# Attention and FFN on one core: score matmuls in two 64-row bf16 tiles, rotating PSUM banks, attention written out

## The chip, the cores and the metric

The program runs on one core of a Trainium2 chip. The metric is device time in microseconds (us). The kernel before takes 944.26 us (median of 3 runs, 941.65 to 945.33).

A core has engines that run side by side: PE (TensorE, matmuls; its weight loads are listed apart as PEld), DVE (VectorE), ACT (ScalarE), POOL (GpSimd) and SP (SyncE, which here only issues DMAs). They meet through semaphores. Matmul results go to PSUM, which has 8 banks of 128x512 f32.

## The reference

One transformer block on x of 32 batches x 256 tokens x 128 features. Attention has 16 heads of 8 features and a distance bias:

```
q, k, v = heads(x @ wq.T), heads(x @ wk.T), heads(x @ wv.T)
attn = softmax(q @ k.T / sqrt(8) - slope[h] * |i - j|)
x = layernorm(x + (attn @ v) @ wo.T + bo)
h = silu(x @ w1.T * s1) * (x @ w2.T * s2)          # 128 -> 512
h = gelu(h @ h1.T * s3); h = gelu(h @ h2.T * s4)   # 512 -> 512
x = layernorm(x + h @ w3.T * s5)
```

## The kernel before

Two stages follow each other: attention over 32 batches, then an FFN over 16 chunks of 512 tokens. The change touches attention alone.

**Stacks.** The scores are matmuls of "stacks". A stack holds for each head a column block whose rows are q and k in split precision (fp32r high and low parts, 3 x 8 rows), rows that build the distance bias, and two rows with the negated maximum of each query. PE projects q and k, ACT and DVE split them into `qk_sb` (the buffer `x_parts` in the profile), SP spills the parts to DRAM (`qk_scratch`) and loads them back as rows of `qk_stack` (L300, L307, L308).

**Two passes per head.** `score_max` (L379, PSUM `ps_a`, 3 banks) makes the scores of the next batch, and DVE takes each query's maximum (L617: a custom add of `corner_rows` with a running minimum, two of 128x256 per head). PE turns the maxima of 8 heads (`turn_max`), ACT and DVE split them (`mrow_hi`, `mrow_lo`), SP writes them as rows of the stack. `score_exp` (L391, `ps_b`, 2 banks) makes the transposed scores of this batch with the maxima subtracted, `add_corner` (L370) adds the part of the bias that the rows can't hold, ACT takes the exponential (L529) into `probs`. `pv` (L406) multiplies 4 heads at once with v in four column tiles of 32; it is fp32 and shows two matmul records per product.

**Order.** It is written out by hand. A step t does 16 slots k: scores-for-maxima of batch t+1, scores-for-exp of batch t, and at the slots in `PE_AT`, `PV_AT`, `ACT_AT`, `DVE_AT` the rest: v projection, q/k projection of batch t+2, turning the output (`turn o`, `turn norm`), `wo`, residual and statistics. `drive` runs steps -2 to 2 written out, 3 to 28 as a loop unrolled by two, the rest written out. POOL adds `bo` and does the layer norm; 11 pieces of FFN weights are split by ACT and DVE during the first and last batches. Two banks `ps_m` serve all these small products.

Of the kernel before, what the change touches and what calls it, by code (L numbers as in the profile page):

```python
# [49 lines left out]
OCOLS = VCOLS // 2  # L50
SLOTS = BLK * HEADS
# [10 lines left out]
STACK = 3 * DH  # L62
MROW = P - 2
KA = MROW
STEPS_T = (MROW - STACK - 4) // BLK // 2 * 2
CORNER = P - STEPS_T
F32_MAX = float(np.finfo(np.float32).max)
QH, QL, KH, KL = range(4)
# [24 lines left out]
ACT_AT = {"max hi 1": 1, "copy o": 2, "v": 3, "qk hi": 4, "max hi 0": 9, "oT": 10}  # L93
DVE_AT = {"max lo 1": 1, "qk lo": 4, "norm": 8, "max lo 0": 10, "res": 13, "stats": 14}
# [7 lines left out]
A_BANK = [1 if h == 3 else (h - 4) % HEADS % 3 for h in range(HEADS)]  # L102


def a_released(b, h):

    before = [g for g in range(h - HEADS, h) if A_BANK[g % HEADS] == A_BANK[h]][-1]
    return b * HEADS + before + 1
# [6 lines left out]

def drive(eng, step, first, loop_from, loop_to, last, unroll):

    for t in range(first, loop_from):
        step(t, t % 2)
    with eng.Fori(0, (loop_to - loop_from) // unroll, 1) as i:  # L120
        for u in range(unroll):
            step(i * unroll + (loop_from + u), (loop_from + u) % 2)
    for t in range(loop_to, last + 1):
        step(t, t % 2)
# [33 lines left out]
def norm_x1(nc, pool, b, par, carried, passed):  # L158
# [3 lines left out]
    wait_apart(pool, carried.stats_done, (b + 1) * BLK, passed)  # L162
# [4 lines left out]
    wait_apart(pool, carried.x1_stored, (b - 1) * DMA, passed)  # L167
# [12 lines left out]

def attention(nc, wts, x, xT, wqT, wkT, wvT, woT, bo, qscale, ident, corner, rows, x1_dram, qk_dram, raw_w, scales,
# [5 lines left out]
    with ExitStack() as ctx:  # L187
# [39 lines left out]
        ps_a = [ctx.enter_context(nc.psum_tensor(f"ps_a{i}", [P, 512], F32)) for i in range(3)]  # L227
        ps_b = [ctx.enter_context(nc.psum_tensor(f"ps_b{i}", [P, 512], F32)) for i in range(2)]
        ps_o = ctx.enter_context(nc.psum_tensor("ps_o", [P, 2, SEQ], F32))
        ps_m = [ctx.enter_context(nc.psum_tensor(f"ps_m{i}", [P, 512], F32)) for i in range(2)]  # L230


        passed = {e: sem(f"passed_{e}") for e in ("sp", "dve", "pool")}
        qk_const_landed = sem("qk_const_landed")
        const_landed = sem("const_landed")
        const_set = sem("const_set")
        rows_landed = sem("rows_landed")
        rows_laid = [sem(f"rows_laid{i}") for i in range(2)]
        v_laid = sem("v_laid")
        xT_landed, x_landed = sem("xT_landed"), sem("x_landed")  # L240
        qk_done, qk_hi, qk_lo = sem("qk_done"), sem("qk_hi"), sem("qk_lo")
        spilled = sem("spilled")
        corner_zero, corner_laid = sem("corner_zero"), sem("corner_laid")
        stacked = [sem(f"stacked{i}") for i in range(2)]
        v_done, v_copied = sem("v_done"), sem("v_copied")
        scores_a, max_done = sem("scores_a"), sem("max_done")
        mT_done, m_hi, m_lo = sem("mT_done"), sem("m_hi"), sem("m_lo")
# [10 lines left out]


        pieces = []  # L260
# [4 lines left out]
        piece_at = [(-2, 8)] * RAW_BUFS + [(0, 11), (1, 11), (2, 11), (BATCH - 3, 11), (BATCH - 2, 11),  # L265
                                           (BATCH - 1, 4), (BATCH - 1, 10)]
        assert len(pieces) == N_PIECES == len(piece_at)

        def pieces_of(t, k):

            return [n for n, (step, head) in enumerate(piece_at) if step == t and k in (None, head)]
# [4 lines left out]
        N_CONST, N_QK_CONST = 5, 3  # L276


        STEPS = dict(first=-2, loop_from=3, loop_to=BATCH - 3, last=BATCH, unroll=2)
        FIRST = STEPS["first"]  # L280

# [764 lines left out]
```

## Time and profile before

| | |
|---|---|
| median of 3 runs | 944.26 us |
| profiled execution, its span | 943.94 us, 942.2 us |
| PE, PEld busy | 892.2 us (95%), 724.7 us (77%) |
| DVE, ACT, POOL busy | 728.5 (77%), 640.1 (68%), 138.3 us (15%) |
| DMA moved | 80.60 MB, mean 86 GB/s |

Busy times are unions of an engine's instructions. A matmul's recorded time holds its pipeline latency, so neighbours overlap, and the distance between the starts of two is what each costs in a stream. The same holds for LDWEIGHTS, DVE and ACT.

### The profile page before, as it was taken

The page shows a single profiled execution, that of the slowest core. Times are in us where ns is not written, and L with a number is a line of the kernel's source. Part 1 is how long each engine was busy: PE and PEld are TensorE (multiplying, and loading weights), DVE is VectorE, ACT ScalarE, POOL GpSimd, SP SyncE. Part 2 cuts the span into 40 slices and gives each one's busy share as a digit, 9 for nine tenths or more (in the row PEclk, how much of TensorE's full clock was granted, in tenths as well). Part 3 has the DMA queues.
Part 4 walks back from the last instruction along what each step waited for, and adds up shares of the span by engine and source line. Part 5 has one row for each costly group of instructions (what it writes and reads, how often), then busy time and mean ns, then how long its engine had stood idle before and what let it go on. Part 6 is the DMA issues. An engine that isn't in the chain of part 4 may idle for free. (4 is left out here: it accounts for less than half of the span.)

```text
span 942.2 us, 23595 instructions
## 1 busy us (share of the span) xinstructions
PE 892.2 (95%) x6786; PEld 724.7 (77%) x6786; DVE 728.5 (77%) x2975; ACT 640.1 (68%) x1136; POOL 138.3 (15%) x213
## 2 busy tenths in 40 slices
PE   2799999999999999999999985999999999999995
PEld 1678878888888888888888863788888888888883
DVE  6788888889888888888988954666677777767664
ACT  5377667666666667666666763677777777777772
POOL 3002121121212112121121312001000000000101
PEclk9799999999999999999999997999999999999998
DMA  6344444344344343444434411001111111111001
GB/s 180 101 116 124 136 112 128 110 113 136 108 130 121 115 126 112 132 113 130 112 112 137 127 48 31 28 23 34 34 33 40 39 45 33 39 39 33 23 23 45
DMA packets 72307, 80.60 MB, mean 86 GB/s; under 512 B 8208, under 2 KB 68368, under 8 KB 69200
## 3 DMA queue, kind: packets, MB, share of 16 engines
q1 hardware_dynamic: 71392, 77.28, 29.1%
q0 software_dynamic: 880, 2.88, 1.0%
q8 instruction: 18, 0.29, 0.1%
q14 instruction: 17, 0.14, 0.0%
HBM read 45.53 MB, written 33.55 MB: 84 GB/s over the span
## 5 line engine op out<-in xcount | busy, mean ns | idle before, releaser
L617 DVE CUSTOM_DVE_ANT_0 scored<-ps_a,corner_rows 128x256 f32<-128x256 f32 x1024 | 376.4, 418 | 16.0 <-PE ps_a L379 6.1
L529 ACT ACTIVATE probs<-ps_b 128x512 f32<-128x512 f32 x512 | 300.0, 598 | 128.0 <-PE ps_b L370 125.7
L379 PE MATMUL ps_a<-qk_stack 126*128 126x256 f32 x1024 | 244.2, 321 | 15.9 <-DMA qk_stack<-qk_scratch 12.8
L391 PE MATMUL ps_b<-qk_stack 128*128 128x256 f32 x1024 | 211.0, 288 | 3.2 <-ACT probs L529 2.4
L379 PEld LDWEIGHTS ps_a<-qk_stack 126*128 126x128 f32 x1024 | 158.9, 193 | 46.5 <-issue 27.4
L391 PEld LDWEIGHTS ps_b<-qk_stack 128*128 128x128 f32 x1024 | 159.0, 191 | 8.3 <-ACT probs L529 4.6
L851 ACT ACTIVATE gelu_f<-ps_r,sc 128x512 f32<-128x512 f32 x128 | 88.2, 689 | 79.9 <-PE ps_r L792 72.4
L406 PE MATMUL ps_o<-probs,v_aug 128*32 128x256 f32 x2048 | 137.0, 385 | 0.4 <-ACT probs L529 0.4
L370 PE MATMUL ps_b<-corner_sb,idr_sb 128*128 128x160 f32 x512 | 122.4, 239 | 0.0
L789 PE MATMUL ps_r<-g1h,h_hi 128*128 128x512 f32 x256 | 102.8, 401 | 1.9 <-DVE g1l L916 1.9
L789 PE MATMUL ps_r<-g2h,h_hi 128*128 128x512 f32 x256 | 102.8, 401 | 0.0
L792 PE MATMUL ps_r<-g1l,h_hi 128*128 128x512 f32 x256 | 102.3, 399 | 0.0
L792 PE MATMUL ps_r<-g2l,h_hi 128*128 128x512 f32 x256 | 101.4, 396 | 0.0
L370 PEld LDWEIGHTS ps_b<-corner_sb,idr_sb 128*128 128x128 f32 x512 | 97.0, 189 | 0.0
L882 DVE TENSOR_TENSOR g2l<-gelu_f,g2h 128x512 fp32r<-128x512 f32 x64 | 44.4, 694 | 59.5 <-ACT g2h L852 59.3
L617 DVE DVE_READ_ACCUMULATOR2_ANT negmax<- 128x1 f32 x1024 | 83.6, 82 | 0.0
L406 PEld LDWEIGHTS ps_o<-probs,v_aug 128*32 128x32 f32 x2048 | 53.4, 109 | 34.3 <-ACT probs L529 0.6
L882 DVE TENSOR_TENSOR g3l<-gelu_f,g3h 128x512 fp32r<-128x512 f32 x64 | 42.9, 690 | 33.6 <-ACT g3h L852 33.6
L163 POOL TENSOR_SCALAR vareps<-meanvar 128x2 f32<-128x2 f32 x32 | 7.3, 228 | 406.7 <-DVE meanvar L647 401.2
L906 DVE SCALAR_TENSOR_TENSOR gate_f<-ps_r,sc,act_f 128x512 f32<-128x512 f32 x64 | 46.0, 749 | 20.8 <-ACT act_f L861 20.3
L789 PEld LDWEIGHTS ps_r<-g1h,h_hi 128*128 128x128 f32 x256 | 48.7, 190 | 14.7 <-DVE g1l L916 3.0
L792 PEld LDWEIGHTS ps_r<-g1l,h_hi 128*128 128x128 f32 x256 | 48.8, 191 | 11.7
(99 smaller groups left out, 1260.5 us busy)
## 6 DMA issues: line engine op xcount, KB each, us to landing
qk_stack<-qk_scratch SPq DMA_DIRECT2D x64, 384.0 KB
qk_scratch<-x_parts SPq DMA_DIRECT2D x32, 512.0 KB, 3.0
qk_scratch<-x_parts SPq DMA_DIRECT2D x32, 256.0 KB, 3.3
xT_sb<-in_xT SPq DMA_DIRECT2D x32, 128.0 KB, 2.1
x_sb<-in_x SPq DMA_DIRECT2D x32, 128.0 KB, 2.5
x_scratch<-x_sb SPq DMA_DIRECT2D x32, 128.0 KB, 1.7
x_in<-x_scratch SPq DMA_DIRECT2D x32, 128.0 KB, 2.1
x_res<-x_scratch SPq DMA_DIRECT2D x32, 128.0 KB, 2.1
```

The costliest lines, as they stand in the source:

```text
L163: nc.gpsimd.tensor_scalar(vareps[:], mv[:, :, 1], EPS, None, ALU.add).then_inc(carried.eps_done, 1)
L370: return pe.matmul(out, idr_sb[:], corner_sb[:], start=False, stop=True, skip_group_check=True)
L379: mm = pe.matmul(ps[:, qb * SEQ:(qb + 1) * SEQ], q_stack[par][0:KA, h, qb * P:(qb + 1) * P], k_stack[par][0:KA, h, :], start=(qb == 0), st ...
L391: pe.matmul(ps[:, kb * SEQ:(kb + 1) * SEQ], k_stack[par][:, h, kb * P:(kb + 1) * P], q_stack[par][:, h, :], start=(kb == 0), stop=False, s ...
L406: mm = pe.matmul(ps_o[VCOLS * g:VCOLS * (g + 1), pack, :], v_flat[:, kb, first:first + VCOLS], probs[:, h % HALF, kb * SEQ:(kb + 1) * SEQ] ...
L529: nc.scalar.activation(probs[:, k % HALF, :], ps_b[k % 2][:], ACT.Exp, scale=slope[k]).then_inc(exp_done, 1)
L617: ins = nc.vector.tensor_tensor_reduce(scored[:, k % 2, qb, :], ps_a[A_BANK[k]][:, qb * SEQ:(qb + 1) * SEQ], corner_rows[:, qb, :], -1.0, ...
L789: pe.matmul(ps[:], w_hi, a_hi, start=(k == 0), stop=False)
L792: mm = pe.matmul(ps[:], w_hi, a_lo, start=False, stop=(k == kt - 1))
L851: nc.scalar.activation(gelu_f[:, o, :], ps_r[o][:], ACT.Gelu, scale=scale)
L882: nc.vector.tensor_tensor(lo[:, o, :], gelu_f[:, o, :], hi[:, o, :].bitcast(F32), ALU.subtract).then_inc(signal, 1)
L906: nc.vector.scalar_tensor_tensor(out=gate_f[:, o, :], in0=ps_r[o][:], scalar=sc[:, 1, o:o + 1], in1=act_f[:, o, :], op0=ALU.mult, op1=ALU. ...
```

## The change

- **Score matmuls.** The stacks become bf16: 6 terms x 8 rows = 48 rows for three-part q and k, 4 bias rows (KA = 52), 2 rows of maxima (KB = 54). They fit into 64 partitions, so heads of even number lie in partitions 0 to 63 and of odd number in 64 to 127 (`GROUPS = 2`, `TILE = 64`). A matmul on one half uses one 64-row tile of PE. The maxima pass and the exp pass of a slot use different halves (`h = k ^ 1`), and their matmuls alternate.
- **Corner.** Both passes now add a bias block by matmul: two of 128 columns per pass and head, with weights `eye_sb`. `corner_rows` and the custom DVE instruction go; DVE does one `tensor_reduce` of 128x512 with `negate` per head.
- **Banks.** `ps_a` 3 and `ps_b` 4 banks rotate over all uses, the small products too; `ps_m` goes. The waits come from `take_a` and `take_b`.
- **Splits.** ACT copies q/k (128x512) and maxima out of PSUM in f32; POOL makes the bf16 parts (four instructions of 128x512 and four of 16x128 per batch, L785 to L800 of the new file). POOL also splits the 11 weight pieces, in steps 2 to 12.
- **DMA.** The spill is 5 DMAs of 512-byte runs instead of 2 of 1-KB runs, the load of a stack 2 of 4-KB runs per part and half; four max-row DMAs instead of two. Four stacks instead of two; q/k are projected 4 batches ahead, and the maxima pass runs 4 heads further ahead (`AHEAD = 4`).
- **Start.** Steps -4 to 33, all written out. The first stack comes in two halves (`stack_first`); maxima of batch 0 are turned at slots 3 and 12, and DVE makes its split itself (`split_first`).

```diff
-PV_AT = (5, 9, 13)
-PE_AT = {"last pv": 1, "turn max 1": 1, "v": 2, "qk": 4, "turn o": 7, "turn max 0": 9, "turn norm": 10, "wo": 12}
+AT = {"v": 0, "wo": 0, "pv 3": 3, "max 0": 6, "turn o": 6, "pv 0": 6, "turn norm": 9, "pv 1": 9, "qk": 11, "max 1": 14, "pv 2": 14}
+def a_slot(t, k):
+    n = k + AHEAD
+    return t + 1 + n // HEADS, n % HEADS
...
+            def score_max(ps, i, h, qb):
+                g, j = h % GROUPS, h // GROUPS
+                rows_of = slice(g * TILE, g * TILE + KA)
+                pe.matmul(ps[:, qb * SEQ:(qb + 1) * SEQ], q_stack[i][rows_of, j, qb * P:(qb + 1) * P],
+                          k_stack[i][rows_of, j, :], start=(qb == 0), stop=False, skip_group_check=True)
...
+            def add_corner(ps, g, turned, sub):
+                rows_of = slice(g * TILE, (g + 1) * TILE)
+                out = ps[:].rearrange("p (b c) -> p b c", c=P)[:, 0:4:3, sub * TILE:(sub + 1) * TILE]
+                return pe.matmul(out, eye_sb[rows_of, sub, :], corner_sb[rows_of, 2 * turned + sub, :, :], start=False,
+                                 stop=True, skip_group_check=True)
...
+                for half in range(BLK):
+                    if in_a:
+                        score_max(to_a, i_a, h_a, half)
+                    if in_b:
+                        score_exp(to_b, s, k, half)
+                for sub in range(2):
+                    if in_a:
+                        mm_a = add_corner(to_a, h_a % GROUPS, 0, sub)
+                    if in_b:
+                        mm_b = add_corner(to_b, (k ^ 1) % GROUPS, 1, sub)
...
-                        for qb in range(BLK):
-                            ins = nc.vector.tensor_tensor_reduce(
-                                scored[:, k % 2, qb, :], ps_a[A_BANK[k]][:, qb * SEQ:(qb + 1) * SEQ], corner_rows[:, qb, :], -1.0, F32_MAX,
-                                ALU.add, ALU.min, negmax[:, k // HALF, k % HALF, qb:qb + 1])
+                        nc.vector.tensor_reduce(negmax[:, h_a // HALF, h_a % GROUPS, h_a % HALF // GROUPS, :],
+                                                ps_a[a_bank(t, k)][:].rearrange("p (b k) -> p b k", b=BLK),
+                                                AX_X, ALU.max, negate=True).then_inc(max_done, 1)
...
+                wait(pool, spilled, (b - 1) * SPILLS * DMA)
+                nc.gpsimd.tensor_copy(parts[:, 0, :, :], qk_f[:]).then_inc(qk_first, 1)
+                wait(pool, qk_first, b + 1)
+                nc.gpsimd.tensor_tensor(qk_rest[:], qk_f[:], parts[:, 0, :, :], ALU.subtract).then_inc(qk_left, 1)
+                wait(pool, qk_left, b + 1)
+                nc.gpsimd.tensor_copy(parts[:, 1, :, :], qk_rest[:]).then_inc(qk_second, 1)
+                wait(pool, qk_second, b + 1)
+                nc.gpsimd.tensor_tensor(parts[:, 2, :, :], qk_rest[:], parts[:, 1, :, :], ALU.subtract).then_inc(qk_split, 1)
```

PE before, in a step of the middle, from `turn o` to the first products with v (L379 maxima pass, L391 exp pass, L370 corner, L421 `turn o`, L406 `pv`, L414 `turn_max`):

```order
156 L421 MATMUL ps_m<-id_sb,o_sb 128x128 x4
157 L379 MATMUL ps_a<-qk_stack 128x256 x2
158 L391 MATMUL ps_b<-qk_stack 128x256 x2
159 L370 MATMUL ps_b<-corner_sb,idr_sb 128x2x80
160 L379 MATMUL ps_a<-qk_stack 128x256 x2
161 L391 MATMUL ps_b<-qk_stack 128x256 x2
162 L370 MATMUL ps_b<-corner_sb,idr_sb 128x2x80
163 L406 MATMUL ps_o<-probs,v_aug 32x256 x8
164 L414 MATMUL ps_m<-id_sb,negmax 16x128
```

PE now, the same place of a step (L515 `turn_max`, L539 `turn_o`, L506 `pv`, L446 and L454 the two passes, L461 the corners):

```order
4025 L515 MATMUL ps_b<-id_sb,negmax 16x128
4026 L539 MATMUL ps_a<-id_sb,o_sb 128x128 x4
4027 L506 MATMUL ps_o<-probs,v_aug 32x256 x8
4028 L446 MATMUL ps_a<-qk_stack 128x256
4029 L454 MATMUL ps_b<-qk_stack 128x256
4030 L446 MATMUL ps_a<-qk_stack 128x256
4031 L454 MATMUL ps_b<-qk_stack 128x256
4032 L461 MATMUL ps_a<-corner_sb,eye_sb 128x2x64
4033 L461 MATMUL ps_b<-corner_sb,eye_sb 128x2x64
4034 L461 MATMUL ps_a<-corner_sb,eye_sb 128x2x64
4035 L461 MATMUL ps_b<-corner_sb,eye_sb 128x2x64
```

A head has 8 matmuls instead of 5, in pairs on different halves, and the small products stand in one bundle every two or three heads instead of singly.

POOL now, one step of the middle (L785, L787 maxima, L794 to L800 the q/k parts, L819 adds `bo`, L198 to L204 the layer norm of a batch). Before, a step of POOL had the last four rows only:

```order
205 L785 CAST mrow<-max_f 16x128
206 L787 TENSOR_TENSOR mrow<-max_f,mrow 16x128
207 L794 CAST qk_sb<-qk_f 128x512
208 L796 TENSOR_TENSOR qk_rest<-qk_f,qk_sb 128x512
209 L798 CAST qk_sb<-qk_rest 128x512
210 L800 TENSOR_TENSOR qk_sb<-qk_rest,qk_sb 128x512
211 L785 CAST mrow<-max_f 16x128
212 L787 TENSOR_TENSOR mrow<-max_f,mrow 16x128
213 L819 TENSOR_TENSOR xb_sb<-x_sb,bo_sb 128x256
214 L198 TENSOR_SCALAR vareps<-meanvar 128x2
215 L200 TENSOR_TENSOR rstd<-vareps,minus_half 128x2
216 L204 TENSOR_SCALAR x_sb<-res,meanvar,rstd 128x128 x2
```

The second pair of maxima rows stands behind the q/k split of a later batch in POOL's queue.

## Rows read from the trace of the kernel before

**Rows 1.** Windows by stage: busy us (instructions) of each engine, PEclk, DMA share, GB/s.
```profile
0.00:37.40 37.40, 13.80 (x51) 10.37 (x52) 24.98 (x87) 12.80 (x15) 7.69 (x17) 0.92 0.57 160
37.40:551.10 513.70, 512.79 (x5047) 423.28 (x5047) 447.86 (x2313) 350.83 (x713) 96.30 (x149) 1.00 0.42 119
551.10:567.90 16.80, 13.96 (x132) 9.86 (x131) 6.92 (x24) 11.97 (x24) 5.79 (x10) 1.00 0.21 57
567.90:573.00 5.10, 2.78 (x27) 1.57 (x27) 1.67 (x4) 1.47 (x3) 1.38 (x2) 1.00 0.25 79
573.00:942.20 369.20, 348.85 (x1535) 279.66 (x1534) 247.11 (x549) 263.07 (x383) 27.18 (x36) 0.97 0.12 34
```

**Rows 2.** Groups of PE and PEld, 200 to 400 us: count | busy, mean ns | idle.
```profile
L379 PE MATMUL ps_a<-qk_stack 126*128 126x256 f32 x387 | 91.7, 318 | 0.0
...
L379 PEld LDWEIGHTS ps_a<-qk_stack 126*128 126x128 f32 x388 | 59.5, 190 | 10.6 <-DVE negmax L617 4.9 <-issue 4.9
L406 PE MATMUL ps_o<-probs,v_aug 128*32 128x256 f32 x768 | 51.4, 385 | 0.0
...
L421 PEld LDWEIGHTS ps_m<-id_sb,o_sb 128*128 128x128 f32 x48 | 5.0, 139 | 0.0
```

**Rows 3.** Timeline from 304 us, PE and PEld: start us, us, instruction.
```profile
304.86 1.07 PE L406 MATMUL ps_o<-probs,v_aug 128*32 128x256 f32 x16
...
305.86 0.30 PEld L379 LDWEIGHTS ps_a<-qk_stack 126*128 126x128 f32 x2
...
306.46 0.52 PEld L456 LDWEIGHTS ps_m<-wv_sb,xT_sb 128*128 128x128 f32 x4
...
306.90 0.30 PEld L379 LDWEIGHTS ps_a<-qk_stack 126*128 126x128 f32 x2
...
307.49 0.30 PEld L379 LDWEIGHTS ps_a<-qk_stack 126*128 126x128 f32 x2
...
308.08 0.30 PEld L468 LDWEIGHTS ps_m<-xT_sb,wq_sb 128*128 128x128 f32 x2
...
308.84 0.41 PEld L379 LDWEIGHTS ps_a<-qk_stack 126*128 126x128 f32 x2
```

**Rows 4.** Groups of DVE and ACT, 200 to 400 us, same columns as rows 2.
```profile
L617 DVE CUSTOM_DVE_ANT_0 scored<-ps_a,corner_rows 128x256 f32<-128x256 f32 x388 | 142.8, 418 | 4.1
L529 ACT ACTIVATE probs<-ps_b 128x512 f32<-128x512 f32 x194 | 113.6, 598 | 45.1 <-PE ps_b L370 44.2
...
L617 DVE DVE_READ_ACCUMULATOR2_ANT negmax<- 128x1 f32 x387 | 31.7, 82 | 0.0
...
L643 DVE BATCH_NORM_STATS2 bn<-res 128x6 f32<-128x128 f32 x24 | 5.8, 286 | 0.4
...
L639 DVE TENSOR_TENSOR res<-ps_m,xb_sb 128x256 f32<-128x256 f32 x12 | 5.0, 420 | 0.0
...
L596 DVE RECIPROCAL recip<-ps_m 128x32 f32<-128x32 f32 x12 | 4.2, 353 | 0.0
...
L647 DVE BATCH_NORM_AGGREGATE meanvar<-bn 128x2 f32<-128x6 f32 x24 | 2.9, 164 | 0.0
```

**Rows 5.** Timeline of the start: DVE reduces, first score matmuls, first exponential.
```profile
16.45 1.26 DVE L655 TENSOR_REDUCE lo_max<-w_lo 128x1 f32<-128x512 f32 x2
...
19.90 1.62 PE L379 MATMUL ps_a<-qk_stack 126*128 126x256 f32 x6 [10.17 <-DMA qk_stack<-qk_scratch]
...
37.44 0.60 ACT L529 ACTIVATE probs<-ps_b 128x512 f32<-128x512 f32 x1 [8.06 <-PE ps_b L370]
```

**Rows 6.** Groups of POOL, 200 to 400 us, same columns as rows 2.
```profile
L169 POOL TENSOR_SCALAR x_sb<-res,meanvar,rstd 128x128 f32<-128x128 f32 x24 | 18.9, 798 | 3.5 <-POOL rstd L165 3.5
L690 POOL TENSOR_TENSOR xb_sb<-x_sb,bo_sb 128x256 f32<-128x256 f32 x12 | 8.8, 737 | 0.0
L165 POOL TENSOR_TENSOR rstd<-vareps,minus_half 128x2 f32<-128x2 f32 x12 | 8.6, 718 | 1.0
```

**Rows 7.** DMA issues: KB each, median us to landing.
```profile
qk_stack<-mrow_lo SPq DMA_DIRECT2D x64, 8.0 KB, 2.8
```

More of the change, by code:

```diff
@@ L60 @@
 DMA = 16
[L62 to L68, printed above, removed]
+PARTS = 3
+MPARTS = 2
+TERMS = 6
+STACK = TERMS * DH
+GROUPS = 2
+TILE = P // GROUPS
+HG = HEADS // GROUPS
+HH = HG // 2
+KA = STACK + 4
+MROW = KA
+KB = KA + MPARTS
+OCOLS = VCOLS // 2
+SLOTS = BLK * HEADS
+SPILLS = 5
+XT_BUFS = 6
 def slopes():
@@ L257, in attention @@
         raw_hi, lo_seen = sem("raw_hi"), sem("lo_seen")
+        FIRST, LAST = -4, BATCH + 1
+        assert all(a_bank(t, use) != 0 for t, use in ((BATCH, "wo"), (BATCH, "turn o"), (BATCH + 1, "wo")))
         pieces = []
@@ L264, in attention @@
                 pieces.append(tuple(w[:, a:a + HID // n, :] for w in (hi, lo, src)))
[L265 to L271, printed above, removed]
+        PIECE_FIRST = 2
+        piece_at = range(PIECE_FIRST, PIECE_FIRST + N_PIECES)
+        assert len(pieces) == N_PIECES
         def raw_piece(n):
@@ L415, in turn_max, with project_v @@
                              id_sb[:]).then_inc(mT_done, 1)
-            def turn_o(b):
-                wait(pe, o_copied, b + 1)
+            def project_v(t):
+                wait(pe, xT_landed, (t + 1) * DMA)
+                ps = take_b(t, "v")
+                for tb in range(BLK):
+                    mm = pe.matmul(ps[:, tb * D:(tb + 1) * D], xT_sb[t % XT_BUFS][:, tb * P:(tb + 1) * P],
+                                   wv_sb[:], start=True, stop=True, skip_group_check=True)
+                mm.then_inc(v_done, 1)
@@ L419, in turn_o, with project_out @@
+            def project_out(t):
+                wait(pe, oT_copied, t - 1)
+                ps = take_a(t, "wo")
+                for qb in range(BLK):
+                    mm = pe.matmul(ps[:, qb * D:(qb + 1) * D], oT_sb[:, qb * P:(qb + 1) * P], wo_sb[:],
+                                   start=True, stop=True, skip_group_check=True)
+                mm.then_inc(wo_done, 1)
+            def turn_o(t):
+                wait(pe, o_copied, t)
+                ps = take_a(t, "turn o")
                 for qb in range(BLK):
@@ L425, in step, with project_qk @@
+            def project_qk(t):
+                wait(pe, xT_landed, (t + 5) * DMA)
+                if t == FIRST:
+                    pe.wait_ge(wq_scaled, 1)
+                ps = take_b(t, "qk")
+                for n, w in enumerate((wqs_sb, wk_sb)):
+                    mm = pe.matmul(ps[:, n * SEQ:(n + 1) * SEQ], w[:], xT_sb[(t + 4) % XT_BUFS][:], start=True, stop=True,
+                                   skip_group_check=True)
+                mm.then_inc(qk_done, 1)
             def step(t, s):
[L426 removed]
+                par = s % 2
+                if t == FIRST + 2:
@@ new lines, in step @@
+                    if k == AT["turn o"] and live(t - 1, BATCH):
+                        turn_o(t)
+                    if k == AT["turn norm"] and live(t - 1, BATCH):
+                        turn_norm(t)
+                    if k == AT["qk"] and live(t + 4, BATCH):
+                        project_qk(t)
+                    if k == AT["pv 3"] and live(t - 1, BATCH):
+                        pv(t - 1, 1 - par, 3)
+                    for j in range(3):
+                        if k == AT[f"pv {j}"] and live(t, BATCH):
+                            pv(t, par, j)
@@ L495, in _ @@
+            for t in range(FIRST, LAST + 1):
+                step(t, t % STACKS)
             pe.wait_ge(ones_set, 1)
@@ L571, in _ @@
+            for dst, src in ((eye_f, eye), (corner_f, corner), (id_sb, ident)):
+                act.dma_start(dst[:], src).then_inc(const_landed, DMA)
+            for t in range(FIRST, LAST + 1):
+                step(t, t % STACKS)
         @block.vector
@@ L697, in ffn @@
+            for t in range(FIRST, LAST + 1):
+                step(t, t % STACKS)
 def ffn(nc, wts, x1_dram, out, carried):
```

675 lines of the change are left out of this document (350 added, 325 removed).

## The prediction

> **What bounds the kernel now.** I cut the span into stages first [rows 1]. The reader is to see PE busy 512.79 of 513.70 us from the first exponential (37.4) to the last batch's (551.1), and 348.85 of 369.20 in the FFN. DVE has 447.86 there, ACT 350.83, DMA a share of 0.42: PE sets the pace. The stretch of 513.7 us is 31 batches of 16.57 us. [...] Around it lie 37.4 us of start, 16.8 us of the last batch, 5.1 us of tail and 369.2 us of FFN; the profiled run is 943.94 us, 1.7 us more than its span and 0.3 us under the median.
>
> Then I read the timeline for what PE spends a batch on [rows 3]. One head (two maxima matmuls, two exp matmuls, one corner) takes 0.59 us from weight load to weight load (306.90 to 307.49 to 308.08), five pairs of load and matmul, 0.12 us each. [...] A group of products with v takes 1.00 us (304.86 to 305.86), four a batch. The v projection takes 0.44 (306.46 to 306.90), the q/k projection 0.76 (308.08 to 308.84). I give `wo` 0.44 like v (same four records), `turn o` 0.42 by the same count, `turn norm` half of it, 0.2, the two turned maxima 0.1 each. So: scores 16 x 0.59 = 9.4; v products 4.0; the rest 0.44 + 0.44 + 0.76 + 0.42 + 0.2 + 0.2 = 2.5; together 15.9. The 0.7 to 16.57 is what PE loses at waits and at changes of tile shape.
>
> **The change part by part.**
>
> *Scores on PE.* A head now has 4 matmuls of 256 columns and 4 of 128, in pairs on different 64-row halves. The trace has no row tile, no bf16 and no such pair. Column tiles it has: a v group is 16 records of 379 to 404 ns that finish in 1.07 us [rows 3], so four tiles do stream at once. [...] The loads are the other limit: 8 a head. An fp32r load of 128 columns is recorded with 190 ns and costs 0.107, so 83 ns of it are latency; the load for a turn is recorded with 139 [rows 2], which leaves 0.055. bf16 has half the bytes of fp32r, so I put it at 0.055. Two loads per pair make 0.11, which a 256-column pair just covers and a 128-column pair doesn't: 4 x 0.11 = 0.44 us a head. Ends: 0.32 (loads hidden) and 0.86 (eight loads at 0.107, none overlapping another). I take 0.44, nearest to the one-pass row: 16 x 0.44 = 7.0 us instead of 9.4.
>
> *The rest of PE* is unchanged in number: 6.5 us. Of the 0.7 us of losses I keep 0.6: the small products are bundled, but leaving the 64-row shape for another and coming back is new for some of them.
>
> [...]
>
> PE per batch: 7.0 + 6.5 + 0.6 = 14.1 us.
>
> *DVE.* Gone are 32 custom instructions of 418 ns with 82 ns reads of the accumulator [rows 4], and the splits. New are 16 reduces of 128x512. Two reduces of that size from SBUF take 1.26 us, 0.6 apart [rows 5]; from PSUM I bound it by 0.60 and 0.69. With residual, statistics, reciprocal and norm (420 + 2 x 286 + 2 x 164 + 353 ns [rows 4], and 420 for the norm, of the residual's size: about 2.1 us): 11.7 to 13.1 us, take 12.2. Below PE's 14.1, so it hides; without PE's bound it would be the next floor.
>
> *ACT.* 16 exponentials of 598 ns, as before [rows 4] (9.6 us at full recorded length), copies of 128x512 twice, 128x256 twice, 16x128 twice: 2.5 us more. 12.1 at most; hidden.
>
> *POOL.* New per batch: two subtracts and two casts of 128x512. A 128x256 subtract-like instruction takes 737 ns [rows 6], so 1.47 us for 512; a cast is bounded by half of that and by all of it. Four: 4.4 to 5.9, take 5.0. Four 16x128 instructions with waits 1.3; `xb` 0.74, rstd 0.72, norm 2 x 0.8, vareps and gaps 0.6. Sum 10.0 us (9.4 to 11.0), in the 11 steps with a weight piece 12.4 to 13.9. It fits under 14.1, barely with a piece. Its slip would show in the max rows: the first pair is turned at slot 6, passes ACT, POOL, four issues and a landing (0.3 + 0.8 + 4 x 0.5 us, my estimates, and 2.8 us of landing [rows 7]) and is wanted 10 slots = 8.8 us later; 3 us to spare.
>
> *DMA.* Bytes stay: spill 12 x 128 x 512 B = 768 KB against 768 KB, stack 768 KB against 768 KB. The rate rises by 16.57/14.1 to 140 GB/s, share 0.5. Three more spill issues and four more row issues a batch are about 3.5 us of SP, which isn't the bound. Cost nothing.
>
> *Start.* The first score matmul is at 19.90 [rows 5], behind constants, split, spill and stack; the first exponential at 37.44. The new order has ACT issue two constants, halves of the first stack, no weight pieces: some 2 us earlier. Then 16 reduces, and 4 of the next batch, 20 x 0.65 = 13 us at most, less idle than the 17.5 us now. I put the first exponential at 32.5 and 2 us of hold-up behind it (rows of the second half queued behind a stack on SP): 34.5 against 37.4; ends 30 and 42.
>
> *Last batch.* No maxima pass: 16 exponentials and four v groups, 12 us for 16.8. Weight pieces are gone from there. *Tail and FFN:* the same chain, 5.1 + 369.2 = 374.3.
>
> **Sum:** 34.5 + 31 x 14.1 (437.1) + 12 + 374.3 = 857.9 us of span, + 1.7 = 859.6. I say 859.
>
> **Rivals.**
>
> *DVE becomes the bound.* If loads hide wholly (0.32 a head), PE has 5.1 + 6.5 + 0.6 = 12.2 and DVE about 12.4: 34.5 + 384.4 + 12 + 374.3 + 1.7 = 807. For it: side-by-side column tiles do work. Against: eight loads in 0.32 us is 0.04 each, under any row.
>
> *POOL or the max rows come late.* If a cast or subtract with bf16 output takes half as much again, POOL has 12.5, 15.5 with a piece, and PE waits at slot 0 or 8: 15.5 a batch on average gives 903.
>
> *The tiles give nothing (slower).* The place is the score pairs. If both halves stream in line, a head is 0.64, PE 10.2 + 6.5 + 0.6 = 17.3 a batch, and the last batch 14: 34.5 + 536.3 + 14 + 374.3 + 1.7 = 961. It decides from 0.60 us a head, where a batch costs 16.7. Against it are the 16 v records in 1.07 us.
>
> *Loads at the fp32r pace (slower).* Eight loads of 0.107 us one after another: 0.86 a head, 20.9 a batch, 34.5 + 647.9 + 17 + 374.3 + 1.7 = 1075. For it: 190 ns is what every 128-column score load takes. Against: 139 ns for the identity.
>
> [...]
>
> *It does not do what it says:* the written-out program could stall on instruction fetch and give back what it wins; nothing in the trace points to it (the FFN and 5 steps are written out or short loops alike). It would land near 940.
>
> **How the numbers follow.** Main case 0.60, DVE bound 0.13, POOL or rows late 0.12, tiles in line 0.08, loads at 0.107 0.05, nothing won 0.02. The main case's own range is 830 to 890 (0.40 to 0.50 us a head, start at its ends). The 8-in-10 range takes in the DVE case and most of the late-rows case: 805 to 920. 0.5% (4.7 us) is what a measurement here can tell from no change. Faster 0.84, within 0.5% 0.03, slower 0.13.
>
> **What would show it.** In the new profile: batch period (every 16 exponentials) near 14.1; eight score loads in about 0.44 us with the second matmul of a pair starting within 0.06 us of the first; PE nearly without idle; DVE about 85% busy, reduces 0.6 to 0.69; POOL about 70%; granted clock 1.00; first exponential at 31 to 35; FFN 369 long. [...]

## The result

The changed kernel takes 852.31 us (median of 4 runs, 851.28 to 858.29) against 944.8 us for the kernel before in the same job; ratio 0.9035, 95% interval 0.8985 to 0.9086. The prediction was 859, with a range of 805 to 920. The profiled execution is 851.28 us with a span of 849.5 us.

### The profile page after: what moved, and what is told of

It is laid out like the page before. It is cut to its first block and busy times, and to the rows that moved or that the text cites. A ratio compares the mean times of both kernels' runs of the same rounds, so it can differ in the third digit from the quotient of the medians.

```text
span 849.5 us, 22838 instructions
## 1 busy us (share of the span) xinstructions
PE 801.8 (94%) x8322; PEld 578.6 (68%) x8322; DVE 633.5 (75%) x1302; ACT 604.8 (71%) x1095; POOL 311.5 (37%) x487
## 2 busy tenths in 40 slices
DMA packets 102173, 81.21 MB, mean 96 GB/s; under 512 B 11840, under 2 KB 94912, under 8 KB 102080
## 3 DMA queue, kind: packets, MB, share of 16 engines
q8 instruction: 63, 1.03, 0.6%
## 5 line engine op out<-in xcount | busy, mean ns | idle before, releaser
L718 DVE TENSOR_REDUCE negmax<-ps_a 128x2 f32<-128x512 f32 x512 | 325.2, 682 | 65.4 <-PE ps_a L461 61.7
L628 ACT ACTIVATE probs<-ps_b 128x512 f32<-128x512 f32 x512 | 271.6, 600 | 106.2 <-PE ps_b L461 105.8
L446 PE MATMUL ps_a<-qk_stack 52*128 52x256 bf16 x1024 | 186.2, 278 | 10.7 <-DVE negmax L718 4.3
L454 PE MATMUL ps_b<-qk_stack 54*128 54x256 bf16 x1024 | 182.5, 273 | 0.4 <-ACT probs L628 0.4
L461 PE MATMUL ps_a<-corner_sb,eye_sb 64*128 64x128 bf16 x1024 | 141.3, 220 | 0.0
L461 PE MATMUL ps_b<-corner_sb,eye_sb 64*128 64x128 bf16 x1024 | 139.0, 216 | 0.0
L506 PE MATMUL ps_o<-probs,v_aug 128*32 128x256 f32 x2048 | 138.1, 387 | 0.1
L446 PEld LDWEIGHTS ps_a<-qk_stack 52*128 52x128 bf16 x1024 | 69.0, 95 | 79.3 <-DVE negmax L718 50.0
L461 PEld LDWEIGHTS ps_a<-corner_sb,eye_sb 64*128 64x128 bf16 x1024 | 97.8, 97 | 9.7
L461 PEld LDWEIGHTS ps_b<-corner_sb,eye_sb 64*128 64x128 bf16 x1024 | 96.2, 95 | 5.3
L506 PEld LDWEIGHTS ps_o<-probs,v_aug 128*32 128x32 f32 x2048 | 53.7, 109 | 42.8 <-issue 13.0
L785 POOL CAST mrow<-max_f 16x128 bf16<-16x128 f32 x64 | 17.9, 280 | 161.0 <-ACT max_f L609 161.0
L454 PEld LDWEIGHTS ps_b<-qk_stack 54*128 54x128 bf16 x1024 | 68.2, 94 | 3.5 <-ACT probs L628 2.7
```

What stands on the lines that cost most here:

```text
L446: pe.matmul(ps[:, qb * SEQ:(qb + 1) * SEQ], q_stack[i][rows_of, j, qb * P:(qb + 1) * P], k_stack[i][rows_of, j, :], start=(qb == 0), stop= ...
L454: pe.matmul(ps[:, kb * SEQ:(kb + 1) * SEQ], k_stack[i][rows_of, j, kb * P:(kb + 1) * P], q_stack[i][rows_of, j, :], start=(kb == 0), stop= ...
L461: return pe.matmul(out, eye_sb[rows_of, sub, :], corner_sb[rows_of, 2 * turned + sub, :, :], start=False, stop=True, skip_group_check=True)
L506: mm = pe.matmul(ps_o[VCOLS * g:VCOLS * (g + 1), pack, :], v_flat[:, kb, first:first + VCOLS], probs[:, h % HALF, kb * SEQ:(kb + 1) * SEQ] ...
L628: nc.scalar.activation(probs[:, h % HALF, :], ps_b[b_bank(t, k)][:], ACT.Exp, scale=slope[h]).then_inc(exp_done, 1)
L718: nc.vector.tensor_reduce(negmax[:, h_a // HALF, h_a % GROUPS, h_a % HALF // GROUPS, :], ps_a[a_bank(t, k)][:].rearrange("p (b k) -> p b k ...
```

## The profile after

The stages: to the first exponential, to the first exponential of the last batch, to the end of the last exponential, 5.1 us of tail, FFN. Columns: busy us and instruction count of PE, PEld, DVE, ACT, POOL, then granted clock, DMA share, GB/s.

```profile
0.00:33.90 33.90, 20.50 (x107) 12.41 (x107) 18.97 (x29) 14.99 (x13) 13.08 (x24) 1.00 0.67 165
33.90:464.05 430.15, 419.91 (x6515) 279.29 (x6516) 363.00 (x709) 315.72 (x678) 263.40 (x419) 1.00 0.63 145
464.05:475.20 11.15, 10.74 (x142) 6.74 (x141) 1.94 (x7) 9.37 (x20) 3.62 (x6) 1.00 0.24 63
475.20:480.30 5.10, 2.93 (x29) 1.68 (x29) 2.53 (x8) 1.61 (x4) 2.34 (x4) 1.00 0.16 51
480.30:849.50 369.20, 347.69 (x1537) 278.45 (x1536) 247.05 (x550) 263.07 (x383) 29.07 (x37) 0.98 0.12 34
```

[rows 1] and the prediction end the middle stage before at 551.10 us. The first exponential of the last batch stands a little later there:

```profile
552.43 1.11 ACT L529 ACTIVATE probs<-ps_b 128x512 f32<-128x512 f32 x2 [0.15 <-PE ps_b L370]
```

So the middle stage is 430.15 us now, 31 batches of 13.88 us, and was 515.0 before, 16.61 each. That is 84.9 of the 92.7 us by which the span fell; the start gives 3.5, the last batch 4.3 (15.5 to 11.2). Tail and FFN are 374.3 us in both. PE is still busy 97.6% of the middle, at a clock of 1.00. POOL rose from 96 to 263 us, DMA's share from 0.42 to 0.63.

One stretch of PE, from the last corners of a slot over the bundle of v and output projection to the first two heads after it (PE rows only; start us, us, instruction):

```profile
300.14 0.21 PE L461 MATMUL ps_b<-corner_sb,eye_sb 64*128 64x128 bf16 x1
...
300.29 0.71 PE L522 MATMUL ps_b<-wv_sb,xT_sb 128*128 128x128 f32 x4
...
300.83 0.61 PE L530 MATMUL ps_a<-wo_sb,oT_sb 128*128 128x128 f32 x4
...
301.38 0.28 PE L446 MATMUL ps_a<-qk_stack 52*128 52x256 bf16 x1
...
301.38 0.28 PE L454 MATMUL ps_b<-qk_stack 54*128 54x256 bf16 x1
...
301.50 0.27 PE L446 MATMUL ps_a<-qk_stack 52*128 52x256 bf16 x1
...
301.50 0.27 PE L454 MATMUL ps_b<-qk_stack 54*128 54x256 bf16 x1
...
301.61 0.22 PE L461 MATMUL ps_a<-corner_sb,eye_sb 64*128 64x128 bf16 x1
...
301.61 0.22 PE L461 MATMUL ps_b<-corner_sb,eye_sb 64*128 64x128 bf16 x1
...
301.67 0.21 PE L461 MATMUL ps_a<-corner_sb,eye_sb 64*128 64x128 bf16 x1
...
301.67 0.21 PE L461 MATMUL ps_b<-corner_sb,eye_sb 64*128 64x128 bf16 x1
...
301.72 0.27 PE L454 MATMUL ps_b<-qk_stack 54*128 54x256 bf16 x1
```

And the weight loads (PEld) of that first head's first four matmuls:

```profile
301.37 0.09 PEld L446 LDWEIGHTS ps_a<-qk_stack 52*128 52x128 bf16 x1
301.38 0.09 PEld L454 LDWEIGHTS ps_b<-qk_stack 54*128 54x128 bf16 x1
301.39 0.10 PEld L446 LDWEIGHTS ps_a<-qk_stack 52*128 52x128 bf16 x1
301.39 0.10 PEld L454 LDWEIGHTS ps_b<-qk_stack 54*128 54x128 bf16 x1
```

Four things are to be seen. The two matmuls of a pair start in the same 10 ns: the halves stream side by side. Pairs follow each other by 0.11 us at 256 columns and 0.06 at 128, so a head costs 0.34 (301.38 to 301.72). The loads of the two halves run at the same time, 0.09 us each. And the bundle costs 1.18 us (corners end near 300.20, next head at 301.38), where v stood among full-height matmuls with 0.44 [rows 3], and the output projection with 0.45 (median of the trace before). Inside the bundle the matmuls start 0.11 us apart, eight of them 0.88. The other 0.3 is at its two ends: 0.09 before the first matmul, 0.21 instead of 0.11 between the first and the second, and again 0.21 from the last to the next head.

The groups from 200 to 400 us (count | busy, mean ns | idle before):

```profile
L718 DVE TENSOR_REDUCE negmax<-ps_a 128x2 f32<-128x512 f32 x233 | 148.1, 682 | 25.8 <-PE ps_a L461 23.9
L628 ACT ACTIVATE probs<-ps_b 128x512 f32<-128x512 f32 x233 | 123.4, 600 | 45.3 <-PE ps_b L461 45.3
L446 PE MATMUL ps_a<-qk_stack 52*128 52x256 bf16 x468 | 83.2, 271 | 0.5 <-issue 0.5
L454 PE MATMUL ps_b<-qk_stack 54*128 54x256 bf16 x468 | 83.0, 271 | 0.0
...
L461 PEld LDWEIGHTS ps_a<-corner_sb,eye_sb 64*128 64x128 bf16 x468 | 44.0, 94 | 3.6
...
L446 PEld LDWEIGHTS ps_a<-qk_stack 52*128 52x128 bf16 x468 | 31.5, 94 | 31.2 <-DVE negmax L718 22.0 <-issue 7.3
...
L796 POOL TENSOR_TENSOR qk_rest<-qk_f,qk_sb 128x512 f32<-128x512 f32 x15 | 17.4, 1157 | 1.2
...
L787 POOL TENSOR_TENSOR mrow<-max_f,mrow 16x128 bf16<-16x128 f32 x29 | 12.1, 417 | 2.4
...
L819 POOL TENSOR_TENSOR xb_sb<-x_sb,bo_sb 128x256 f32<-128x256 f32 x14 | 10.0, 717 | 0.0
...
L798 POOL CAST qk_sb<-qk_rest 128x512 bf16<-128x512 f32 x15 | 9.1, 609 | 1.0
```

A bf16 load of 128 columns stands with 94 ns against 190 for fp32r [rows 2]. DVE's reduce takes 682 ns, the exponential 600 as before [rows 4], POOL's casts about 0.6 and subtracts 1.16 us.

I added up PE's stretches over 200 to 400 us from such starts, 14 or 15 batches. Mean us from the end of the corners to the next head, and what I had assumed for the same work:

```
bundle                              measured  assumed
slot 0   v, output projection        1.18      0.88
slot 3   pv                          1.13      1.00
slot 6   max, turn o, pv             2.06      1.52
slot 9   turn norm, pv               1.46      1.20
slot 11  q/k                         1.15      0.76
slot 14  max, pv                     1.30      1.10
together                             8.28      6.46
16 heads (29 pairs, 58 triples)      5.5       7.0
```

8.28 + 5.5 = 13.8 is the period. These are means. By medians slot 3 is 1.09, slot 6 is 2.00 and three heads are 1.01, all else as above, and a batch is 13.60: most batches take 13.60 us to a hundredth, and a few take 1 to 3 us more. The first two (14.75 and 16.81) lose 4.4 us together, behind holes of 1.9 and 2.0 us in front of a head at 39.8 and 54.6 us. Later holes stand also inside groups of matmuls that, by the profile, wait for nothing. This is the third and the fourth of the four matmuls of one `turn o`:

```profile
180.93 0.52 PE L539 MATMUL ps_a<-id_sb,o_sb 128*128 128x128 f32 x3
182.74 0.27 PE L539 MATMUL ps_a<-id_sb,o_sb 128*128 128x128 f32 x1 [1.28 <-issue]
```

The trace has three such holes inside a group of more than 0.3 us, 2.6 us in all; the trace of the kernel before, whose middle steps are a loop, has none. More on them behind the experiments.

## The experiments

The kernel before was run beside each; its medians were 944.2 to 945.8 us, so absolute times compare. Repeats of one kernel spread by 0.5 to 1.5% here (the changed kernel's own four by 0.8%), so two medians that differ by less than 8 us say little. The distance between the first exponentials of two batches in the traces is sharper. Its mean is the length of the middle stage over 31; its median leaves the holes out:

```
run                           time (median)  batch: mean  median
kernel before                    944.80        16.61      16.59
changed kernel                   852.31        13.87      13.60
both passes on one half          937.18        16.97      16.65
lighter DVE                      855.34        14.05      13.34
no corners                       835.92        13.41      13.00
four ps_a banks, three ps_b      864.84        14.33      14.05
one visit more                   857.37        13.92      13.70
one visit fewer                  859.96        14.04      13.85
two visits fewer                 870.10        14.48      14.29
start as it was                  857.84        13.88      13.60
corner weights of 127 columns    855.49        14.09      13.64
more work for POOL               855.36        14.01      13.60
turns at 9 and 12                858.29        13.94      13.55
turns at 9 and 11                860.09        14.12      13.54
```

**Both passes on one half.**

```diff
-                h = k ^ 1
+                h = k
...
-                        mm_b = add_corner(to_b, (k ^ 1) % GROUPS, 1, sub)
+                        mm_b = add_corner(to_b, k % GROUPS, 1, sub)
```

> The maxima pass and the exp pass of a slot are put on the same 64-row half; nothing else changes in number. My theory (the halves stream side by side, 0.33 us a head): two passes on one half must follow each other, so a head costs about 0.66, PE gains 16 x 0.33 = 5.3 us a batch, and of the 2 us that PE waits now about 1.5 are swallowed: period 13.9 to 17.6, time about 852 + 31 x 3.7 = 967 (range 940 to 1010). Rival (the gain over the kernel before comes from bf16 and one-pass loads, and both halves would be pipelined anyway): period stays under 14.5, time under 875.

Measured: 937.18 us (934.95 to 948.62), ratio to the kernel before 0.9907 (0.9886 to 0.9929). The timeline of its PE, one head and the start of the next:

```profile
301.46 0.28 PE L446 MATMUL ps_a<-qk_stack 52*128 52x256 bf16 x1
...
301.58 0.27 PE L454 MATMUL ps_b<-qk_stack 54*128 54x256 bf16 x1
...
301.69 0.27 PE L446 MATMUL ps_a<-qk_stack 52*128 52x256 bf16 x1
...
301.80 0.27 PE L454 MATMUL ps_b<-qk_stack 54*128 54x256 bf16 x1
...
301.92 0.22 PE L461 MATMUL ps_a<-corner_sb,eye_sb 64*128 64x128 bf16 x1
...
301.92 0.28 PE L446 MATMUL ps_a<-qk_stack 52*128 52x256 bf16 x1
...
301.97 0.21 PE L461 MATMUL ps_b<-corner_sb,eye_sb 64*128 64x128 bf16 x1
...
302.04 0.27 PE L454 MATMUL ps_b<-qk_stack 54*128 54x256 bf16 x1
```

On one half the passes follow each other by 0.11 us. 85 us, nine tenths of the whole gain, goes with it, and the median batch is as long as in the kernel before, 16.65 us against 16.59. (Four of the six times lie at 935 to 938 us, two at 948.5; the trace is of one of these two, and its first two batches take 25.5 and 21.5 us.) But a head costs 0.46, not 0.66: while the corners of one head run (301.92), the next head, on the other half, has begun. Two heads take 1.15 and three 1.61 us instead of 0.69 and 1.03. So the side-by-side halves are shown to be what pays in the scores; my number for this run (967) was 30 too high, since I had not seen that neighbours in the queue overlap whenever their halves differ.

**A lighter DVE.** The reduce reads half of the keys.

```diff
-                                                ps_a[a_bank(t, k)][:].rearrange("p (b k) -> p b k", b=BLK),
+                                                ps_a[a_bank(t, k)][:].rearrange("p (b k) -> p b k", b=BLK)[:, :, 0:P],
...
-                                             scale=slope[h]).then_inc(exp_done, 1)
+                                             scale=slope[h] * 1e-3).then_inc(exp_done, 1)
```

> DVE reads 128 of the 256 keys of each query for the maximum (so the maxima are those of half the keys, and the exponentials are taken with a scale 1000 times smaller to stay finite; both change values only). A reduce falls from about 0.65 to 0.38 us, DVE by 4.3 us a batch. If PE's waits for ps_a banks that DVE holds are what lies between PE's own work (about 12 us) and the period of 13.9: period 12.5, time 852 - 31 x 1.4 = 809 (795 to 825). Rival (PE's own work with changes of tile shape is the 13.9, DVE is hidden as I predicted): within 5 us of 852.

Measured: 855.34 us (852.86 to 857.82). As a forecast of the time the theory fell; a small part of it is true all the same. The page had led me to it: these are the waits of the changed kernel, 200 to 400 us (us in total, times, longest):

```profile
PEld ps_a L446 <- DVE negmax L718: 22.0, 54, 0.4
PEld ps_a L446 <- issue: 7.3, 20, 0.6
```

and the same two of this run:

```profile
PEld ps_a L446 <- issue: 22.9, 57, 0.8
...
PEld ps_a L446 <- DVE negmax L718: 7.0, 17, 0.4
```

Its window from 200 to 400 us, the columns as in the table of stages:

```profile
200.00:400.00 200.00, 194.12 (x3048) 130.35 (x3046) 110.79 (x331) 146.93 (x316) 119.96 (x192) 0.99 0.63 145
```

DVE fell from 171 us to 111 of 200, and the idle time only changed its name, from "DVE negmax" to "issue" (22.0 + 7.3 against 7.0 + 22.9 us). Most of it (58 times 0.41 us, 24 of the 29 us) is behind a v group: the load of the next head begins only when the group is nearly through. In the kernel before, the same 0.41 us stand behind every v group. So this wait isn't DVE's.

But the median batch fell from 13.60 to 13.34 us. All of that is in slot 6, where the bundle with `turn o` takes 1.74 us instead of 2.00: `turn o` takes a ps_a bank and waits 0.26 us for the reduce that still holds it. With both passes on one half, where DVE has more time, it is 1.74 us as well, and without corners the wait stands under its own name:

```profile
PE ps_a L534 <- DVE negmax L713: 7.1, 15, 0.5
```

(L534 is `turn o` there.) DVE costs 0.26 us a batch, 8 us in all. The time doesn't show it: the trace of this run has more holes inside groups, 11.0 us in six places. DVE is hidden but for that.

**No corners.** The four corner matmuls of each head are left out (and the second score matmul of a pass ends the accumulation in their place).

```diff
-                for sub in range(2):
-                    if in_a:
-                        mm_a = add_corner(to_a, h_a % GROUPS, 0, sub)
-                    if in_b:
-                        mm_b = add_corner(to_b, (k ^ 1) % GROUPS, 1, sub)
```

> The four corner matmuls of each head are left out (so the bias near the diagonal is missing). PE has 0.11 us less a head, 1.8 us a batch. If PE alone bounds: period 12.1, time 852 - 31 x 1.8 = 796. If DVE's reduces bound together with PE through three banks: period 13.0 to 13.4, time 825 to 840. If DVE alone bounded: 850.

Measured: 835.92 us (835.35 to 839.81), 16 less. Its window from 200 to 400 us:

```profile
200.00:400.00 200.00, 186.87 (x2269) 99.14 (x2272) 179.20 (x355) 158.40 (x339) 126.14 (x203) 1.00 0.68 153
```

Two corner pairs of 0.055 us a head are 16 x 0.11 = 1.8 us of PE's work a batch; the period fell by about 0.5 (16 us in 31 batches; 0.6 by the medians). DVE is now at 90%, PE at 93%. So the next floor lies close: PE can save about half a microsecond a batch before it meets DVE and the banks (which of the two would give way first, no run here tells). The bundle with `turn o` grew to 2.46 us, PE waiting there.

**Four ps_a banks, three ps_b.**

```diff
-A_BANKS, B_BANKS = 3, 4
+A_BANKS, B_BANKS = 4, 3
```

(and `ps_a[2]` instead of `ps_a[0]` for the FFN's first tokens).

> ps_a gets 4 banks and ps_b 3. If PE loses time because three banks hold too little work for DVE during the bundles of small products (1 to 2 us each): period 13.2 to 13.6, time 830 to 843. If the exp side needs its fourth bank as much: 852 or above, up to 870. If banks are not what PE waits for: 852 within 3.

Measured: 864.84 us (861.62 to 872.49), 12 more. PE now waits before a bundle: 0.35 us at slot 6 and 0.30 at slot 9 instead of 0.09, where the small product needs one of the three ps_b banks. 3 and 4 is the better split; the exp side needs its fourth bank because five of the small products live there (both turned maxima, v, `turn norm`, q/k), as I read it.

**One visit more, one and two fewer.** In the first only PE's slot moves; in the other two ACT's and DVE's parts move too where they hang on it.

One more:

```diff
-..., "turn norm": 9, "pv 1": 9, ...
+..., "turn norm": 8, "pv 1": 9, ...
```

> The turn of the normalised output goes one slot earlier, so PE leaves the 64-row shape seven times a batch instead of six; no work is added. Theory A (each visit of another shape costs PE 0.25 to 0.35 us, about 1.8 us a batch in all, which the prediction left out): period +0.3, time +8 to +11 us. Rival B (shape changes cost nothing beyond the 0.09 us before a bundle; PE's extra time in bundles is waiting for data): time within 3 us of the changed kernel.

One fewer:

```diff
-..., "qk": 11, "max 1": 14, "pv 2": 14}
+..., "qk": 14, "max 1": 14, "pv 2": 14}
```

> The q/k projection moves from slot 11 to slot 14, into the bundle with the second turned maxima and the products with v: five visits instead of six. Theory A: period -0.3, time -8 to -10 us, unless the longer bundle (2.2 us) lets DVE and ACT run dry. Rival B: no change.

Two fewer, q/k as in the last one and besides:

```diff
-AT = {"v": 0, "wo": 0, "pv 3": 3, ...
+AT = {"v": 3, "wo": 3, "pv 3": 3, ...
```

> As the run before, and the v projection and the output projection move from slot 0 to slot 3, with the last products with v: four visits. Theory A: period -0.5 to -0.6, time -16 to -18 us, less what DVE's own 12.3 us a batch takes back: I expect 838 to 843. Rival B: no change, or slower, since two bundles of over 2 us drain three ps_a banks of 0.65 us each: 855 to 865.

Measured: 857.37 (852.81 to 864.89), 859.96 (858.22 to 862.13), 870.1 us (866.64 to 874.87). In the timelines the turn alone costs 0.46 us and the v group behind it 1.09, together 1.55 against 1.46 in one bundle: 0.09 for the visit, not 0.3. A turn is 0.2 us of matmuls, so 0.26 is paid wherever it stands. As I read it, that is the change of tile shape: `pv` has a shape of its own (column tiles of 32), and in a bundle with it PE changes shape as often as between bundles. No run changes the shape alone. Merging q/k into slot 14 did save, 2.17 for 1.30 + 1.15; but the five heads in a row that it leaves take 2.24 us instead of 1.71, since DVE gives banks back every 0.61, and the first exponential comes at 37.0 instead of 33.9. Moving v and `wo` to `pv` saved only 0.09 (2.18 for 1.18 + 1.09) and left a second run of five heads. Theory A was right in that a visit costs (0.09 us), wrong in that fewer visits save time: what PE saves, it then waits for banks. For the run with one more visit 857 against 852 can't be told from no change, but its median batch is longer by 0.10, the 0.09 of the visit.

**The start as it was.** First stack whole, maxima at slots 6 and 14, rows behind the spill.

```diff
-                if t == -1:
-                    max_rows(0, 0, 0)
...
-                    if t + 3 == 0:
-                        stack_first(0)
-                        stack_first(1)
-                    else:
-                        stack((s + 3) % STACKS, 1 - par)
+                    stack((s + 3) % STACKS, 1 - par)
...
-                    if k == (3 if t < 0 else AT["max 0"]) and live(t + 1, BATCH):
+                    if k == AT["max 0"] and live(t + 1, BATCH):
...
-                    if k == (AT["qk"] + 1 if t < 0 else AT["max 1"]) and live(t + 1, BATCH):
+                    if k == AT["max 1"] and live(t + 1, BATCH):
```

> The new order of the first batches is undone: the first stack comes whole, the maxima of batch 0 are turned at slots 6 and 14, and their rows stand behind the spill of batch 2 on SP and its split on POOL. The prediction gave the start 3 us in all. If these two edits make it: first exponential 37 to 40 instead of 33.9, time +3 to +6. Rival (the start is earlier by ACT's own constants and the missing weight pieces alone): within 1.5 us.

Measured: 857.84 us (855.63 to 860.22), 5.5 more. The first exponential of the changed kernel (start us, us, instruction, idle before it):

```profile
33.92 0.60 ACT L628 ACTIVATE probs<-ps_b 128x512 f32<-128x512 f32 x1 [2.14 <-PE ps_b L461]
```

and the first of this one:

```profile
38.83 0.60 ACT L620 ACTIVATE probs<-ps_b 128x512 f32<-128x512 f32 x1 [5.03 <-PE ps_b L455]
```

4.9 of the 5.5 us are there, and the median batch is the same, 13.60. So the two edits are the whole gain at the start; without them this kernel would start 1.4 us later than before [rows 5].

**Corner weights of 127 columns.**

```diff
-                out = ps[:].rearrange("p (b c) -> p b c", c=P)[:, 0:4:3, sub * TILE:(sub + 1) * TILE]
-                return pe.matmul(out, eye_sb[rows_of, sub, :], ...
+                out = ps[0:P - 1].rearrange("p (b c) -> p b c", c=P)[:, 0:4:3, sub * TILE:(sub + 1) * TILE]
+                return pe.matmul(out, eye_sb[rows_of, sub, 0:P - 1], ...
```

> The weights of the corner matmuls are cut from 128 to 127 columns (so the last query or key of 128 gets no corner bias). [...] Rival (any bf16 load is fast): 94 ns and 852.

Measured: 855.49 us (852.99 to 858.6), no change that the times can tell. Its load group:

```profile
L461 PEld LDWEIGHTS ps_a<-corner_sb,eye_sb 64*127 64x127 bf16 x458 | 55.8, 134 | 2.5 <-issue 0.7
```

134 ns instead of 94: one column fewer makes the load 40 ns longer. Yet two heads still take 0.68 us and three 1.06 (0.69 and 1.03 before the edit). I had put this run at about 905 us, with the longer loads setting the pace. So the loads are not the limit even at 134 ns, and the prediction's two loads of 0.055 in a row per pair did not occur; the loads of the two halves run beside each other, as the matmuls do. (Both loads of a corner pair start at 302.08 us in this run's trace, 0.13 us each.)

**More work for POOL.** Three spare casts of 128x512 ahead of the split.

```diff
+                nc.gpsimd.tensor_copy(spare[0][:], qk_f[:])
+                nc.gpsimd.tensor_copy(spare[1][:], qk_f[:])
+                nc.gpsimd.tensor_copy(spare[2][:], qk_f[:])
                 nc.gpsimd.tensor_copy(parts[:, 0, :, :], qk_f[:]).then_inc(qk_first, 1)
```

> POOL does three more casts of 128x512 per batch, 1.8 us, ahead of the q/k split. The prediction said 3 us to spare. If so: within 4 us of 852, except that the eleven steps with a weight piece may slip. If POOL is near the bound: +1.8 us x 31 = +56.

Measured: 855.36 us (853.79 to 864.05). POOL's 1.8 us per batch, 56 in all, cost 3 us at most. The median batch is the same, 13.60. POOL is hidden with at least that to spare.

**A better order?** Both turns moved, `turn norm` to the projection of q/k; ACT's copy and DVE's `normalise` move with them.

```diff
-..., "turn o": 6, "pv 0": 6, "turn norm": 9, "pv 1": 9, "qk": 11, ...
+..., "turn o": 9, "pv 0": 6, "turn norm": 12, "pv 1": 9, "qk": 12, ...
```

> The turn of the output goes from slot 6 to 9, the turn of the normalised output from 9 to 12, beside the q/k projection (also 12); both turns then stand beside work of their own tile shape, and PE does not wait for ACT's copy of the output. Theory (PE's own time in the bundles, changes of shape in it, is the bound): the bundles 2.06 + 1.46 + 1.15 us become about 1.30 + 1.55 + 1.45, period -0.3 to -0.4, time 840 to 845. Rival (DVE, now 85% busy, takes it back): 849 to 853.

```diff
-..., "turn o": 6, "pv 0": 6, "turn norm": 9, "pv 1": 9, "qk": 11, ...
+..., "turn o": 9, "pv 0": 6, "turn norm": 11, "pv 1": 9, "qk": 11, ...
```

> As the run before with the normalised turn and q/k at slot 11, which leaves DVE only two slots for the norm. Theory: 840 to 848, a little over the run before if PE then waits for the norm. Rival: 850 or more.

Measured: 858.29 (854.86 to 863.8) and 860.09 us (856.98 to 861.91). In the first, `turn norm` with q/k took 1.33 us, as forecast, but `turn o` with `pv` 1.91, of which 0.34 is a wait before it (0.09 elsewhere), for one of the three ps_a banks, as I read it; no run tells that apart. The bundles sum to 8.13 instead of 8.18 us (medians), and the median batch followed, 13.55 and 13.54 against 13.60. That is 2 us in all; the first trace loses more in its start (first exponential at 35.4) and its first batches (19.67 us the first), the second in holes inside groups (8.7 us). No other order beat the changed kernel's time.

**The holes.** The matmul that is late in the two lines of the last section is number 2273 of the program's 8322. It is late in eight of the twelve traces of the changed program whose matmuls keep this count (all but the run without corners), by 1.2 to 3.2 us. Here is the lighter DVE:

```profile
180.61 0.49 PE L539 MATMUL ps_a<-id_sb,o_sb 128*128 128x128 f32 x3
183.84 0.27 PE L539 MATMUL ps_a<-id_sb,o_sb 128*128 128x128 f32 x1 [2.73 <-issue]
```

In the two runs with other turns number 2273 is a product with v, and it is late there too. The others that are late again and again are numbers 577, 1425, 3121, 3969, 4817 and 5665, each 848 further, which is four batches. So the place in the program decides and not the work. The DMA queue by the name of instruction moved this, first before and then now (packets, MB, share of 16 engines' span):

```profile
q8 instruction: 18, 0.29, 0.1%
q8 instruction: 63, 1.03, 0.6%
```

I take these holes for PE waiting for its own instructions, which the written-out program has more of. No run tests it. They cost 2.6 us in the trace of the changed kernel and 11.0 in the lighter DVE's, none in two others, and they differ from run to run, so they hide or feign differences of some us between two medians.

## Why the prediction was right

The forecast was 7 us high, and its mechanism held: PE sets the pace, the row halves stream side by side, POOL, ACT and DMA stay hidden, DVE too but for 0.26 us a batch, the FFN doesn't move. But two terms of the sum were mis-sized and nearly cancelled: 1.5 us a batch too much for the scores, 1.2 too little for the rest with its losses (7.1 against 8.3). That the time came out within 1% is luck in that part.

- *Scores on PE* (0.44 us a head taken, 0.32 and 0.86 the ends): 0.34. The load term was wrong. I had let the two loads of a pair follow each other; they overlap, and each is recorded with 94 ns. 1.5 us a batch too much, 46 in all. The 0.107 of an fp32r load is near the measured one: two stand as 0.30 us and one as 190 ns [rows 2, 3], so 0.11. But no run shows 0.055 as what a bf16 load costs by itself, since none sets the pace. Nor does any run show the lower end of 0.32 or its double, 0.64: with the passes on different halves a head costs 0.34, with both on one half 0.46.
- *The rest of PE* (6.5 us and 0.6 of losses): 8.28. I had carried the small products over from among matmuls of their own full-height shape. Now each stands between 64-row matmuls or beside `pv`, and they cost 1.8 us a batch more than the 6.5. Of this 0.26 is `turn o` waiting for DVE, and some 0.1 are holes. About 1.4 is left, and I put it on the changes of tile shape, an estimate. It fits that the projection of q/k, four records of 256 columns in a row, takes 0.76 us before, and a v group, four in a row on each of its four column tiles, 1.00 [rows 3]; and that `turn norm` costs less beside q/k than beside `pv` (0.18 against 0.37 us).
- *DVE* (12.2 us): busy 11.8 a batch, reduces of 682 ns, at the top of the 0.60 to 0.69 range. Hidden but for the 0.26 us that the lighter reduce showed.
- *ACT* (12.1 at most): 10.2. *POOL* (10.0): 8.5 averaged over all batches. The subtract of 128x512 was bounded at 1.47 and took 1.16.
- *DMA* (share 0.5): 0.63. The runs are shorter: 102173 packets instead of 72307 for the same 81 MB. It cost nothing that I can see.
- *Start* (first exponential at 32.5, 2 us of hold-up behind it): 33.9 and 4.4, the hold-up in the first two batches and thus inside the middle stage. The term is 3.8 us short. *Last batch* (12): 11.2. *Tail and FFN* (374.3): 374.3.
- *Middle stage* (31 x 14.1 = 437.1): 430.15, that is 31 x 13.60 = 421.6, the 4.4 of the first two batches and some 4 net of holes and shorter last batches. The prediction cut the stage before at 551.10 us instead of 552.43; this moves its 16.57 to 16.61 and enters no term of its sum.

Of the rivals, DVE as the bound was far nearer than its 0.13 says: with PE 1.8 us lighter the period fell by only 0.5. The case "it does not do what it says" came true in small, if the holes are what I take them for: the stall that the prediction feared, with some us and not with the whole gain. The two slower ones fell: the tiles do stream together, which by the run on one half is worth 85 us, and no load cost 0.107 on the path: the records of bf16 loads are 94 ns long, shorter than that. Nor did the 134 ns of the 127-column loads lengthen a head.

## What to carry over

When matmuls are moved to row tiles, count the small full-height products around them anew: here a bundle of them took 0.1 to 0.5 us more than the same work had taken among full-height matmuls (1.18 us against 0.88 at slot 0, 1.15 against 0.76 at slot 11). Put full-height products beside each other and not beside column-tiled ones: `turn norm` cost 0.18 us beside the q/k projection (1.33 against 1.15) and 0.37 beside `pv` (1.46 against 1.09). Let neighbours in PE's queue use different halves; that was 85 of the 92 us of gain, and it helps in part even when the order is not ideal (a head at 0.46 us and not 0.66 with both passes on one half). A wait that the profile puts on a buffer's reader may not be the reader's: the 0.41 us behind a v group stayed when the reduce was halved. Make the reader faster once before believing it. Then compare the median batch and not the time alone: here the time said that nothing had changed, and the batch showed the 0.26 us that was the reader's.

## What was not expected of the hardware

- Cutting a bf16 weight load from 128 to 127 columns made it longer, 134 against 94 ns.
- Two halves overlap not only in a pair but across heads: with both passes on one half a head cost 0.46 us, less than the 0.66 of its matmuls in line (four starts 0.11 us apart, four 0.055).
- A four-bank/three-bank split the wrong way round costs 12 us of 852 although no engine is busier for it (from 200 to 400 us PE 195 us against 198, DVE 168 against 171).
- PE stands still for up to 3.2 us inside a group of matmuls that, by the profile, wait for nothing, at the same numbered matmuls of the program in kernels that differ.
